# A four-stage block on 64 sequences: four kinds of PSUM use filled with two batches per bank

## The reference

```python
x = x + _L0_xattn_ref(_layernorm(x, axis=-1), ctx_1024, ctx_1024, ...)  # mLSTM cell, 4 heads of 64
x = x + _L0_ffn_ref(_layernorm(x, axis=-1), L0_ffn_weight)              # ternary weight, 256 x 256
x = x + _L1_xattn_ref(_layernorm(x, axis=-1), ctx_1024, L1_xattn_Wq, L1_xattn_Wkv)
x = x + _L1_ffn_ref(_layernorm(x, axis=-1), ...)                        # gated, inner size 1024, quantised
```

## Time and profile before

| what | value |
|---|---|
| median of 3 runs | 816.94 us (810.99 to 819.92) |
| the profiled execution | 810.74 us, of which 808.9 us are its span |
| granted PE clock, mean | 0.972 |
| PE busy, share of the span | 713.7 us, 88% |
| DVE busy | 610.2 us, 75% |
| ACT busy | 584.3 us, 72% |
| POOL busy | 425.2 us, 53% |

### The profile page before, as it was taken

One profiled execution on the slowest core, in us unless ns is written; L12 is line 12 of the kernel. 1 busy time (PEld: TensorE's weight loads), 2 busy tenths in 40 slices (PEclk: granted clock), 3 DMA queues, 4 the chain that ended last, 5 costly groups with the idle time before them and its releaser, 6 DMA issues.

```text
span 808.9 us, 16362 instructions
## 1 busy us (share of the span) xinstructions
PE 713.7 (88%) x4942; PEld 528.2 (65%) x4942; DVE 610.2 (75%) x1620; ACT 584.3 (72%) x1298; POOL 425.2 (53%) x629
## 2 busy tenths in 40 slices
PE   3877989989999899998998989984678899999996
PEld 2675776767768677676776776863435566666664
DVE  4584867877778778786787877875468799999995
ACT  2455677777877778777787787773656788888885
POOL 6653545545446364554655545544034566666665
PEclk9889999999999999999999999997799999999999
DMA  9101102121121211211202111100412233433421
GB/s 300 39 2 53 52 28 79 33 74 53 39 78 39 65 52 39 86 36 60 78 13 91 52 39 52 39 14 27 130 52 70 82 109 94 124 88 110 128 65 61
DMA packets 72622, 55.06 MB, mean 68 GB/s; under 512 B 20093, under 2 KB 72318, under 8 KB 72582
## 3 DMA queue, kind: packets, MB, share of 16 engines
q1 hardware_dynamic: 64134, 50.37, 19.7%
q10 hardware_dynamic: 8448, 4.20, 1.8%
HBM read 29.39 MB, written 20.97 MB: 62 GB/s over the span
## 4 chain that ended last, share of the span: by engine, by line
PE 43%; DVE 32%; ACT 12%; issue 7%; POOL 3%; DMA 1%; SPq 0%; DVEq 0%; ACTq 0%; POOLq 0%
PE bank L609 10%; DVE st L1018 8%; PE bank L574 8%; PE bank L559 7%; PE bank L626 5%; ACT nrm L702 4%; PE bank L582 4%; PE bank L567 4%; DVE C L1221 3%; DVE x L1163 3%; PE bank L618 3%; DVE hh L1176 2%; DVE x L1179 2%; DVE hmax L1224 2%; DVE mv L1021 2%
## 5 line engine op out<-in xcount | busy, mean ns | idle before, releaser
L609 PE MATMUL bank<-WGU,fqT 128*128 128x512 bf16 x512 | 126.1, 386 | 12.2 <-ACT D L808 5.1
L894 POOL TENSOR_TENSOR rs<-ve,minus_half 128x4 f32<-128x4 f32 x64 | 79.7, 1246 | 86.5 <-DVE ve L1024 85.1
L702 ACT ACTIVATE nrm<-x,shift,rs 128x256 f32<-128x256 f32 x128 | 66.5, 590 | 46.6 <-POOL shift L901 44.9
L567 PE MATMUL bank<-ident,nrm 128*128 128x128 f32 x256 | 55.0, 303 | 50.9 <-ACT nrm L702 44.0
L1221 DVE SCALAR_TENSOR_TENSOR C<-bank,fback,D 128x1024 f32<-128x1024 f32 x64 | 82.1, 1284 | 17.8 <-ACT D L808 12.6
L909 POOL TENSOR_SCALAR_AFFINE_SELECT D<-D 128x512 f32<-128x512 f32 x64 | 41.1, 666 | 100.1 <-ACT D L740 100.1
L609 PEld LDWEIGHTS bank<-WGU,fqT 128*128 128x128 bf16 x512 | 48.9, 99 | 65.8 <-DVE C L1221 15.8
L923 POOL TENSOR_TENSOR hh<-us,head_scale 128x256 f32<-128x256 f32 x64 | 44.0, 697 | 82.6 <-ACT usq L764 82.6
L808 ACT ACTIVATE D<-bank,fback 128x1024 f32<-128x1024 f32 x64 | 71.3, 1114 | 21.0 <-PE bank L609 20.2
L812 ACT ACTIVATE fhT<-bank 128x1024 f16<-128x1024 f16 x64 | 65.5, 1023 | 21.6 <-PE bank L618 20.8
L1224 DVE TENSOR_REDUCE hmax<-C 128x1 f32<-128x1024 f32 x64 | 78.1, 1220 | 2.2
(11 more groups left out here) (174 smaller groups left out, 1693.0 us busy)
## 6 DMA issues: line engine op xcount, KB each, us to landing
out_dram<-x SPq DMA_DIRECT2D x32, 512.0 KB, 3.0
xg<-in_x_dram SPq DMA_DIRECT2D x16, 512.0 KB, 3.3
cg<-in_ctx_dram SPq DMA_DIRECT2D x16, 512.0 KB, 3.4
rows_q<-fq ACTq DMA_DIRECT2D x16, 256.0 KB, 2.3
xg<-out_dram SPq DMA_DIRECT2D x8, 512.0 KB, 4.6
cg<-out_dram SPq DMA_DIRECT2D x8, 512.0 KB, 4.9
raw<-in_L_ffn_w_gate_dram SPq DMA_DIRECT2D x1, 1024.0 KB, 8.0
x<-in_L_ffn_w_up_dram SPq DMA_DIRECT2D x1, 1024.0 KB, 10.5
```

Source lines behind the costliest of these rows:

```text
L567: mm = pe.transpose(o[:, c * P:(c + 1) * P], nrm[:, b, c * P:(c + 1) * P], ident[:, :])
L609: mm = pe.matmul(ps[k + half], fqT[:, s, c, :], WGU[:, c, which, half * 512:(half + 1) * 512], start=(c == 0), stop=(c == EC - 1))
L702: act.activation(nrm[:, b, :], src[:, b, :], ACT.Identity, scale=rs[i][:, b:b + 1], bias=shift[i][:, b:b + 1]).then_inc(done, 1)
L894: pool.tensor_tensor(rs[i][:, :], ve[i][:, :], minus_half[:, 0:GB], ALU.pow).then_inc(rstd[i], 1)
```

## The change

In T1, T2, WT and O two batches now share a bank. PE fills the two halves one after the other and marks the bank full with the second. ACT copies both halves of T1, T2 and WT in one instruction: two per group of 512 columns in place of four of 256 (T1, T2), and two of 256 in place of four of 128 (WT). F0, SC and O wait for the copy of the pair, O once per pair. DVE still makes x3 in four instructions, now two from one bank; the second of a pair waits for the first by a new semaphore, `x3_half`, and frees the bank. The uses per full turn fall from 48 to 40, five rounds of the ring, and most uses after T1 lie in other banks than before.

```diff
 SUMS, WEIGHTS = {"WS"}, {"W0", "WG", "WU", "WD"}
-USES = {"UA": 2, "UB": 2, "TT": 2, "GA": 1, "MB": 1, "WS": 1, "W0": 1, "WG": 2, "WU": 2, "WD": 2}
+USES = {"T1": 2, "T2": 2, "WT": 2, "O": 2, "UA": 2, "UB": 2, "TT": 2, "GA": 1, "MB": 1, "WS": 1, "W0": 1, "WG": 2, "WU": 2, "WD": 2}
 
...
         maxed = sem("maxed")
+        x3_half = sem("x3_half")
         exped = sem("exped")
...
                         for b in range(GB):
-                            o = open_(stage, b)
+                            if b % 2 == 0:
+                                o = open_(stage, b // 2).rearrange("p (k n) -> p k n", k=2)
                             pe.wait_ge(nrm_ready[stage == "T2"], GB * z + b + 1)
                             for c in range(EC):
-                                mm = pe.transpose(o[:, c * P:(c + 1) * P], nrm[:, b, c * P:(c + 1) * P], ident[:, :])
-                            shut(mm, stage, b)
+                                mm = pe.transpose(o[:, b % 2, c * P:(c + 1) * P], nrm[:, b, c * P:(c + 1) * P], ident[:, :])
+                            if b % 2 == 1:
+                                shut(mm, stage, b // 2)
                     if stage == "F0":
...
                             o = open_("F0", b)
-                            moved("T1", b)
+                            moved("T1", b // 2)
                             for c in range(EC):
...
                             o = open_("SC", b)
-                            moved("T2", b)
+                            moved("T2", b // 2)
                             for c in range(EC):
...
                         for b in range(GB):
-                            o = open_("WT", b)
+                            if b % 2 == 0:
+                                o = open_("WT", b // 2)
                             moved("SC", b)
-                            shut(pe.transpose(o[:, 0:P], ew[:, b, :], ident[:, :]), "WT", b)
+                            mm = pe.transpose(o[:, b % 2 * P:(b % 2 + 1) * P], ew[:, b, :], ident[:, :])
+                            if b % 2 == 1:
+                                shut(mm, "WT", b // 2)
                     if stage == "O":
                         for b in range(GB):
-                            o = open_("O", b)
-                            moved("WT", b)
-                            shut(pe.matmul(o[:, 0:E], ewT[:, b, :], vg[p][:, b, 0:E],
-                                           start=True, stop=True), "O", b)
+                            if b % 2 == 0:
+                                o = open_("O", b // 2)
+                                moved("WT", b // 2)
+                            mm = pe.matmul(o[:, b % 2 * E:(b % 2 + 1) * E], ewT[:, b, :], vg[p][:, b, 0:E],
+                                           start=True, stop=True)
+                            if b % 2 == 1:
+                                shut(mm, "O", b // 2)
 
...
                     if stage in ("T1", "T2"):
-                        for b in range(GB):
-                            o, done = filled(stage, b)
-                            act.activation((x1T if stage == "T1" else x2T)[:, b, :], o[:, 0:E], ACT.Copy).then_inc(done, 1)
+                        for i in range(GB // 2):
+                            o, done = filled(stage, i)
+                            act.activation(flat(x1T if stage == "T1" else x2T)[:, 2 * i * E:(2 * i + 2) * E], o[:, :],
+                                           ACT.Copy).then_inc(done, 1)
                     if stage == "MB":
...
                     if stage == "WT":
-                        for b in range(GB):
-                            o, done = filled("WT", b)
-                            act.activation(ewT[:, b, :], o[:, 0:P], ACT.Copy).then_inc(done, 1)
+                        for i in range(GB // 2):
+                            o, done = filled("WT", i)
+                            act.activation(flat(ewT)[:, 2 * i * P:(2 * i + 2) * P], o[:, 0:2 * P], ACT.Copy).then_inc(done, 1)
                     if stage == "TT":
...
                     for b in range(GB):
-                        o, done = filled("O", b)
-                        dve.scalar_tensor_tensor(out=x3[:, b, :], in0=o[:, 0:E], scalar=einv[:, b:b + 1],
-                                                 in1=x2[:, b, :], op0=ALU.mult, op1=ALU.add).then_inc(done, 1)
-                    moved("O", GB - 1)
+                        o, done = filled("O", b // 2)
+                        if b % 2 == 1:
+                            dve.wait_ge(x3_half, GB // 2 * z + b // 2 + 1)
+                        ins = dve.scalar_tensor_tensor(out=x3[:, b, :], in0=o[:, b % 2 * E:(b % 2 + 1) * E],
+                                                       scalar=einv[:, b:b + 1], in1=x2[:, b, :],
+                                                       op0=ALU.mult, op1=ALU.add)
+                        if b % 2 == 0:
+                            ins.then_inc(x3_half, 1)
+                        else:
+                            ins.then_inc(done, 1)
+                    moved("O", GB // 2 - 1)
                     dve.sem_inc(x3_ready, GB)
```

## The result

The changed kernel takes 831.01 us (median of 4 runs, 828.76 to 832.06) where the kernel before takes 815.35 (4 runs, 810.99 to 819.92): a ratio of 1.019, 95% interval 1.013 to 1.025. The direction and the range of the prediction (819 to 834) hold; the forecast of 11.1 us more was 4.6 us too low against the 15.7 of the medians. The profiled execution has a span of 826.9 us, 18.0 above that of before.

What follows compares the result with a forecast made beforehand. The prediction took one trip around the dependences, not a full engine, to bound the kernel. 15 turns of 0.66 us and 1.2 in the last made 11.1 us more, from 816.94 to 828.0 us; range 819 to 834.

Steps and rivals of the forecast that it cites:

- What bounds the kernel: Whole loop: no engine is full; a turn of 33.0 us lasts one trip around the loop of dependences.
- T1 and T2: Copies ahead of F0 and SC: the wider first copy makes each start 0.21 us later per turn.
- Rival (a): F0 and SC: PE's transposes release them, copies are hidden and only x3 pays; 821 us, chance 0.12.
- x3: DVE's four x3: two waits on the one before cost 0.12 us each, 0.23 per turn.
- The two instructions that prepare the waits: DVE's queue at x3: they can run under the x3 before them, taken as zero.
- WT, O and the ring: Paired ewT copies and O, and the ring of banks: cost nothing while other work covers O.
- The sum: Whole kernel: 0.66 us per turn, 15 turns giving 9.9, plus 1.2 in the last, together 11.1 us.
- the last turn's 1.2 us: Last turn, O uncovered: 0.45 for O, 0.06 for ewT, 0.23 for x3's waits, 0.42 for F0 and SC.
- the bounds given for it: Added time over the whole kernel: 0.4 to 0.9 us per turn, 7 to 15 us with the last turn's extra.
- the forecast's own range: Time of the changed kernel: 824 to 832 us around 828.0, chance 0.67.
- rival (c): SC of batch 2 also late, or x3's waits at their upper bound: some 0.4 us more per turn; 834, chance 0.15.
- Rival (b): ACT's order of work releases the next stage: its saved 0.37 us per turn shortens the trip; 811 us, chance 0.06.

Runs made afterwards that it cites:

- F0 late: Kernel before, with only F0 waiting for the copy of its pair's second batch; 829.95 us, ratio 1.015.
- SC late: Kernel before, with only SC waiting for the copy of its pair's second batch; 829.31 us, ratio 1.017.
- x3's waits alone: Kernel before, with every odd x3 waiting for the even one ahead of it; 829.80 us, ratio 1.019.
- the ring alone: Changed kernel without x3's waits, T1 and T2 copied in halves; shared banks, ring of 40 and pairs of WT and O kept; 815.21 us, ratio 0.999.
- both together: Changed kernel with T1 and T2 copied in halves and x3's waits replaced by one wait for all four and two increments; 823.04 us, ratio 1.010.
- narrow copies: Changed kernel with T1 and T2 copied in halves again, x3's waits and ring of 40 kept; 822.33 us, ratio 1.009.
- free x3 behind wide copies (both attempts): Changed kernel without waits between x3: banks freed after the last, 830.93 us; or PE waiting for the even ones, 829.60 us.
- the three versions with a shorter turn: Kernel before with x1T of batch 0 earlier, 815.85 us; keyT 0 ahead of gexp, 816.67; both plus nrm of x1 earlier and x3's statistics later, 806.98.

## Why the prediction was right in its sign and short in its size

**What bounds the kernel.** Right. Two edits that take work from nobody but let F0 or SC wait 0.27 us lengthen every turn by 0.27, and two that move one copy shorten it. ACT's saved time brought nothing.

**T1 and T2.** Right: 0.21 + 0.21 forecast, 0.39 measured by undoing both (33.65 to 33.26). F0's start behind its copy's start grew by 0.23. SC's grew by 0.15, a term mis-sized by 0.06: before, SC's weights came 0.11 us after the end of the first copy (247.83 against 247.72), after, 0.05 us (252.72 against 252.67). So SC had not waited for that copy alone. The other candidate is PE's own transposes of T2, which stand just ahead of it and would hide a part of the wider copy; no run tested this. The wide copies took 582 and 585 ns, as keyT. Rival (a), copies hidden, falls.

**x3.** Right: 0.23 forecast, 0.26 to 0.27 measured, the step of a dependent pair being the right price. The two instructions that prepare the waits are inside that figure and can have cost 0.04 at most.

**WT, O and the ring.** Right for the turns of the loop: nothing, shown by the run that kept only them (32.99 us a turn).

**The sum.** The trip was sized well: 0.66 us a turn forecast, 0.67 in the profile, and 11.1 us in all against a remainder of 11.8. Of the last turn's 1.2 us, 1.0 lies behind the start of F0; the profile has 1.6 there, of which 0.2 is F0 itself (5.81 us against 5.58, both at a low clock), so that this term is neither borne out nor refuted.

The step that failed is the sum itself, "15 x 0.66 = 9.9": it held the longer trip to be the whole cost. The clock had been read as 1.00 in the turn of before, and no term stood for its falls in a turn of another length. 6.2 us of the 18.0 in the profile are falls.

That the time still lies in the range is in part luck. The added time is above the bounds given for it, 7 to 15 us: 15.7 by the medians, 18.0 by the profiles. On the 816.94 that the forecast was built on, 15.7 more would be 832.6, past the forecast's own range of 824 to 832; the stated range reached to 834 only because of rival (c), whose two reasons did not occur.

The Trainium skill, Perfetto Trace Analysis, Matmul Optimizations, says that the matmul engine scales its power with use, so that back-to-back matmuls matter. The runs agree only in part, for PE was busy 30.8 of 33.6 us: with F0 late the fall comes in F0, right behind the longer pause, and with SC late in SC; but with x3's waits alone it comes in SC, where PE's pause has hardly grown (1.14 for 1.07).

**Rival (b)**, ACT's time counts, falls: 96 instructions of ACT fewer, and the kernel is slower; with only the ring and the pairs of WT and O left, which still saves 32 of them, there is no gain. **Rival (c)** put 834 down to SC of batch 2 or to dearer x3 waits; the time came near it, but for another reason. The turn shows neither: SC runs on without a gap once started (2.05 us in the timeline, 2.02 before), and x3 took 1.92 us, not the 2.1 of (c).

## What to carry to other kernels

Where no engine is full, follow one trip around the dependences and price an edit by what it does to the start of the next piece on it: fewer and wider copies save the copying engine time and make the first reader wait longer, which here cost 0.2 us a place and turn. Hand a shared bank over in halves if its first half has a reader waiting; sharing itself was free. A gain or loss of a few tenths of a us per turn should be read from turns without a fall of PE's clock and the falls counted by themselves, since they can be as large as the effect.

## What the runs showed of the hardware that I had not expected

The clock of TensorE fell inside the loop with PE busy 30.8 of 33.6 us. In the profiles of turns of 33.0 us (the kernel before, and the ring alone) no turn of the loop had a fall. At 33.28 every second turn had one (F0 late or SC late), at 33.2 and 33.27 three (both together, narrow copies), at 33.38 six, at 33.43 five, at 33.6 and 33.65 five and four, and with shorter turns, 32.15 to 32.5, 32.7 and 32.82, three, three and four. Most cost 1.6 to 1.7 us.

The mean granted clock of all executions says the same: it was 0.966 to 0.968 for each set of the kernel before (17 to 19 executions) and 0.966 for the ring alone (10), but 0.954 to 0.957 with F0 late, with SC late, with free x3 behind wide copies (both attempts) and in the changed kernel (4 each), and 0.961 to 0.963 for the three versions with a shorter turn (6 to 10). So the kernel before has a turn that meets no fall, and both a small loss and a small gain were answered by falls: 4 us added on the trip came out as 13 to 15, and 4 us saved came out as nothing.

Every delay on the trip makes PE idle longer somewhere, and the falls in the loop come in F0 or in the stretch of T2, SC and UA, behind the pauses around T1 and T2 that all these kernels have. The longest pause of PE in the loop of any of these profiles is 1.4 us. Whether it is the length of the turn as such, or where in time its pauses come to lie, is not settled, nor why 33.0 us is good and its neighbours are bad: the runs show that the added pause need not be near the fall, and not how the chip decides.

A wait of DVE on the x3 just issued cost 0.13 to 0.14 us each, and 0.2 in the form that waits on the bank's counter (33.43 against 33.01 us a turn for two). One wait for all four with two increments behind it delayed the statistics by 0.2 us (0.34 against 0.13 behind the x3), most of what the two waits that it replaced had cost.
